# Attention values and router logits in one product per tile beside the shared expert, values kept in DRAM, queries in three half slots

## The reference

```python
xn = layernorm(x)
q = xn @ Wq.T + bq; k = xn @ Wk.T + bk; v = xn @ Wv.T + bv       # per batch
z = softmax(q @ k.T / 16) @ v
gates = softmax(xn @ Wg.T); scores, inds = top_k(gates, 2); scores /= sum(scores)   # 16 experts
y = sum over the two of scores * (silu(xn @ We_gate.T) * (xn @ We_up.T)) @ We_down.T   # hidden 128
shared = (silu(xn @ Ws_gate.T) * (xn @ Ws_up.T)) @ Ws_down.T     # hidden 512
return x + z + y + sigmoid(xn @ Wsg.T) * shared
```

## Time and profile before

| | |
|---|---|
| median of 3 runs | 512.84 us (512.59 to 513.53) |
| the profiled execution | 512.95 us |
| its span | 511.1 us |
| TensorE busy | 503.8 us, 3410 matmuls |
| VectorE, ScalarE, GpSimd busy | 402.7, 279.5, 200.1 us |
| transfers | 71.28 MB, mean 139 GB/s |
| granted TensorE clock | 1.00 in every stretch |

### The profile page before, as it was taken

How to read it: one execution, slowest core, us unless ns; L and a number is a source line. 1 busy time by engine, 2 the same in 40 slices (tenths; PEclk the granted TensorE clock), 3 DMA queues, 4 the chain that set the end, 5 groups by cost and what they waited for, 6 DMA issues and landing times.

```text
span 511.1 us, 10075 instructions
## 1 busy us (share of the span) xinstructions
PE 503.8 (99%) x3410; PEld 462.0 (90%) x3411; DVE 402.7 (79%) x847; ACT 279.5 (55%) x466; POOL 200.1 (39%) x178
## 2 busy tenths in 40 slices
PE   8999999999999999999999999999999999999997
PEld 7898988888989999999999888989989898989986
DVE  5989457899997687777776389897969797888896
ACT  4787885246655464555555547464727364545641
POOL 0001021111005777777770451353554544362730
PEclk9999999999999999999999999999999999999999
DMA  8937176111113565786675730731262213131311
GB/s 311 410 117 280 82 294 233 50 45 39 56 63 114 176 195 182 235 291 195 196 142 148 253 120 25 218 97 53 84 203 98 60 62 84 42 92 32 94 43 63
DMA packets 31185, 71.28 MB, mean 139 GB/s; under 512 B 5312, under 2 KB 9792, under 8 KB 30112
## 3 DMA queue, kind: packets, MB, share of 16 engines
q1 hardware_dynamic: 23840, 51.80, 28.2%
q0 software_dynamic: 6864, 18.75, 14.3%
q10 hardware_dynamic: 432, 0.09, 0.1%
HBM read 43.34 MB, written 27.28 MB: 138 GB/s over the span
## 4 chain that ended last, share of the span: by engine, by line
PE 85%; DVE 7%; issue 4%; DMA 1%; POOL 1%; ACT 1%; POOLq 0%; DVEq 0%
PE ps L805 52%; PE ps L1015 10%; PE ps L945 7%; PE ps L811 6%; PE ps L1047 5%; PE ps L900 1%; PE ps L858 1%; DMA blk_x<-rows,row 1%; POOL rows_y L792 1%; DVE sil L1409 1%; DVE probs_f L1672 1%; PE ps L909 1%; DVE place_hot L1520 1%; DMA rows_y<-ytab,slot 1%; POOL blk_x L762 1%
## 5 line engine op out<-in xcount | busy, mean ns | idle before, releaser
L792 POOL DMA_INDIRECT rows_y<-ytab,slot x64 | 81.0, 1265 | 85.5 <-DVE acc L1687 67.4
L762 POOL DMA_INDIRECT blk_x<-rows,row x79 | 86.0, 1089 | 47.8 <-DVE row L1535 23.3
L805 PE MATMUL ps<-vv,pT 128*128 128x258 f32 x768 | 95.8, 283 | 2.1 <-DVE pT L1331 2.1
L805 PEld LDWEIGHTS ps<-vv,pT 128*128 128x128 f32 x768 | 94.7, 189 | 3.5 <-DVE pT L1331 2.5
L805 PE MATMUL ps<-xT,shared_w 128*128 128x512 f32 x384 | 92.6, 394 | 0.4 <-DVE sil L1409 0.3
L805 PEld LDWEIGHTS ps<-xT,shared_w 128*128 128x128 f32 x384 | 70.7, 188 | 15.5 <-issue 0.8
L805 PE MATMUL ps<-qT,xbT_hi 128*128 128x512 f32 x256 | 79.1, 390 | 0.0
L1015 PE MATMUL ps<-expert_w,blk_xT 128*128 x474 | 66.1, 288 | 0.4 <-DVE blk_xT L1331 0.4
L1015 PEld LDWEIGHTS ps<-expert_w,blk_xT 128*128 128x128 f32 x474 | 59.0, 190 | 0.6 <-issue 0.6
L1319 ACT ACTIVATE probs_f<-probs_f 128x1024 f32<-128x1024 f32 x32 | 33.8, 1056 | 42.6 <-DVE probs_f L1672 42.6
L1125 ACT ACTIVATE scored_t<-ps 128x1024 f32<-128x1024 f32 (+1 forms) x33 | 32.3, 996 | 43.7 <-PE ps L805 39.5
(11 more groups left out here) (166 smaller groups left out, 859.2 us busy)
## 6 DMA issues: line engine op xcount, KB each, us to landing
ytab<-blk_y SPq DMA_DIRECT2D x40, 256.0 KB, 2.7
keys<-xT SPq DMA_DIRECT2D x8, 1024.0 KB, 6.0
stage_e<-in_experts SPq DMA_DIRECT2D x16, 384.0 KB, 3.1
rows<-xn SPq DMA_DIRECT2D x8, 512.0 KB, 3.1
xbT_hi<-keys SPq DMA_DIRECT2D x8, 512.0 KB, 6.1
xbT_lo<-keys SPq DMA_DIRECT2D x8, 512.0 KB, 6.9
out<-acc SPq DMA_DIRECT2D x32, 128.0 KB, 1.7
acc<-in_x SPq DMA_DIRECT2D x7, 512.0 KB, 9.1
```

Source lines behind the costliest of these rows:

```text
L762: e.indirect_dma_start(out=blk_x[:, q, n, :], out_offset=None, in_=rows, in_offset=bass.IndirectOffsetOnAxis(ap=row[:, 2 * b + n:2 * b + n ...
L792: e.indirect_dma_start(out=rows_y[:, r, k, :], out_offset=None, in_=ytab, in_offset=bass.IndirectOffsetOnAxis(ap=slot[:, k, i:i + 1], axis=0),
L805: ins = e.matmul(dst, stationary(p, k), moving(q, k), start=(n == 0), stop=(n == total - 1))
```

## The change

Values and logits come out of one product for each tile of 128 tokens, while the chunk's `xT` is there for the shared expert: the new step `vals` has the tile of `xT` stationary and `value_w` moving, 256 value columns and the router's 18 (16 experts, the shared gate, one for a shift), 274 in all, 6 matmuls into one turn bank. ScalarE copies the 18 logits to their place and the 256 value columns, high part, to `vals_out`; VectorE writes the low part; SP stores both (256 KB) in DRAM. `vals_out` has three places, so ScalarE's copy of a tile waits for the store of the tile three before. `vals_load` brings 2 MB of values per batch into `vv`. What goes: the products `logits`, `logits_turn`, `values_first` and `values` with their copies, remainders and additions, `w_v`, and the clearing of the padded router. New once: `value_w` is split (ScalarE and VectorE, 548 columns), its load of 256 KB stands on SP ahead of the third gate-and-up weight (the load of the same weights late in stage 2 goes).

The queries are kept in three slots of half a batch, so `heads` stands two groups ahead throughout; both halves of batch 0 are made before the first score. In the last two groups the addition of tile 28's rows moves from group 6 into group 7, and two more steps move later. GpSimd's gathers take the bound of their indices from a register that is set once. The DRAM transfers at the start of attention are: shift 0, keys of batch 1 (2 MB), values of batch 0 (2 MB), shift 1, values of batch 1 (2 MB).

```diff
     beside = {
-        0: ([("router_split",), ("root", 1), ("stats", 2)], [("weights_hi", 3), ("invert", 1)], []),
-        1: ([("norm", 1), ("weights_lo", 3)], [("logits", 0)], []),
+        0: ([("root", 1), ("stats", 2)], [("weights_hi", 3), ("invert", 1)], []),
+        1: ([("norm", 1), ("weights_lo", 3)], [("value_split",)], [("keys_store", 0)]),
         2: ([], [("tokens_in", 1)], [("weights_lo", 4), ("weights_hi", 4), ("stats", 3)]),
-        3: ([], [], [("stats", 4)]),
+        3: ([], vals(0, 0, 1), [("stats", 4), ("keys_store", 1)]),
         4: ([("weights_lo", 5)],
-            [("logits", 1), ("logits_turn", 0), ("weights_hi", 5), ("root", 2, 3), ("invert", 2, 3)],
+            [*vals(0, 2, 3), ("weights_hi", 5), ("root", 2, 3), ("invert", 2, 3)],
             []),
-        5: ([("logits_turn", 1), ("best_experts", 0)], [], []),
+        5: ([], vals(1, 0, 1, 2, 3), []),
...
-        13: ([], [("tokens_in", 4)], [("norm", 5), ("expert_split", 1)]),
-        14: ([], [("logits", 4)], []),
-        15: ([("norm", 6)], [("tokens_in", 5)], [("expert_split", 2)]),
-        16: ([], [("tokens_in", 6), ("norm", 7)], []),
+        13: ([], [*vals(3, 2, 3), ("tokens_in", 4)], [("norm", 5), ("expert_split", 1)]),
+        14: ([], vals(4, 0, 1), [("keys_store", 4)]),
+        15: ([("norm", 6)], [*vals(4, 2, 3), ("tokens_in", 5)], [("expert_split", 2)]),
+        16: ([], [*vals(5, 0, 1), ("tokens_in", 6), ("norm", 7)], [("keys_store", 5)]),
...
-    ahead = {1: split("heads", 1, 1), 2: split("heads", 2, 0), 3: split("heads", 2, 1), 4: split("heads", 3, 0),
-             5: split("heads", 3, 1), 6: split("values", 3, 1)}
-    behind = {2: split("values", 1, 1), 3: split("values", 2, 0), 4: split("values", 2, 1), 5: split("values", 3, 0)}
+    ahead = {g: split("heads", *divmod(g + 2, 2)) for g in range(1, GROUPS - 2)}
...
-            steps += [*split("heads", 0, 1), ("heads", 1, 0), ("tops", g), ("heads_split", 1, 0),
-                      ("values", 0, 1), *spread(g), ("values", 1, 0), ("less", new),
-                      ("values_split", 0, 1), ("less", new + 1), *spread_second(g), ("probs", new), ("values_split", 1, 0),
-                      ("less", new + 2), ("probs_hi", new), ("probs", new + 1), ("probs_hi", new + 1), ("probs_lo", new),
-                      ("less", new + 3), ("probs_lo", new + 1), *rows(new + 2), *rows(new + 3)]
+            steps += [("tops", g), *split("heads", 1, 0), *spread(g), ("less", new), ("probs", new), ("less", new + 1),
+                      *spread_second(g), ("probs_hi", new), ("probs", new + 1), ("probs_lo", new), ("less", new + 2),
+                      ("probs_hi", new + 1), ("less", new + 3), ("probs_lo", new + 1), *rows(new + 2), *rows(new + 3)]
...
+                elif kind == "vals":
+                    c, n = a
+                    if (c, n) == (0, 0):
+                        e.wait_ge(value_w_lo, 1)
+                    if n == 0:
+                        e.wait_ge(xT_lo, KD * (c + 1))
+                    product(ps[:, turn_bank(("vals", c, n)), 0:VRC], lambda p, k: xT_of(c)[:, p, k, n * P:(n + 1) * P],
+                            lambda q, k: value_w[:, q, k, :], valued)
...
+                elif kind == "vals":
+                    t = CT * a[0] + a[1]
+                    bank = before[("vals", *a)][0]
+                    e.wait_ge(valued, t + 1)
+                    copied(logits_sb[:, t, :], ps[:, bank, D:VRC], logits_copied)
+                    if t >= VR:
+                        e.wait_ge(vals_stored[t % VR], 16 * (t // VR))
+                    copied(vals_out[:, t % VR, HI, :], ps[:, bank, 0:D], vals_hi)
```

263 lines of the change are left out of this document (115 added, 148 removed).

## The result

The changed kernel takes **519.05 us** (median of 4, 518.05 to 519.70), the kernel before beside it 513.18: ratio **1.0117**, 95% interval 1.0101 to 1.0132. It is slower. The forecast was 513.8, between 508.0 and 518.5: the time lies above the range, by 0.55 at its top, and 5.25 above the middle case.

What follows compares the result with a forecast made beforehand. TensorE, busy 99%, was taken as the bound. Terms -8.7 (work), +6.6 (hand-offs), -0.5 (routing), +3.4 (group 0) and +0.2 (tail) sum to +1.0, giving 513.8 us, range 508.0 to 518.5.

Steps and rivals of the forecast that it cites:

- TensorE's work: Whole kernel: logits, their turns and values go, the 274-column product comes at 0.127 us per matmul; -8.7 us.
- Rival D: New value-and-logit product: 274 columns cost as 258, 1.4 us less, 512.4; a third likely, inside the forecast's case.
- Hand-offs in the shared expert: Shared expert: TensorE waits for banks held until VectorE's remainder is done; +6.6 us, bounds 0 to 13.
- The walk: Shared expert and tail: stepping through the engines' order with measured durations to place and size TensorE's waits; +6.6 in the shared expert.
- Routing and blocks: Routing and start of the blocks: VectorE loses 8 additions and TensorE's small waits may go; -0.5 us, bounds -1 to +2.
- Register: GpSimd's gathers: holding the index bound in a register saves GpSimd's issue at most; 0 us.
- Group 0: Start of attention: TensorE waits 2.7 us for the first pT, plus 0.25 and 0.45 at two hand-offs; +3.4, ends 0 and +5.5.
- The clock: Whole kernel: granted clock taken as 1.00 in every row of stretches, so no term for it.
- Tail: Last groups: shorter group 6 makes score copies of group 7 reach into TensorE; net +0.2 us, bounds -1.5 to +2.
- A: Shared expert, faster: hand-offs hide and the 6.6 falls away, 507.2, or 510.5 if half hidden; chance 0.35.
- B: Start of attention, slower: the burst of 6 MB of loads delays the gathers, 516.5 to 520; chance 0.15.
- C: Two banks and a ring of three too few throughout: stores take 6 us, gaps double to 13, 520.3; chance 0.07.

Runs made afterwards that it cites:

- no_low_read: Changed kernel with the values' low part computed from the high part alone, so a bank is free after ScalarE's copy: 532.90 us, ratio 0.9949 to the kernel before.
- rows_behind: Changed kernel with the row additions of tiles 0 and 1 moved from between group 0's score maxima to behind its last pT: 536.16 us, ratio 1.0017.
- rows_28_back: Changed kernel with tile 28's row additions back at the end of group 6, as before the change: 534.29 us, ratio 1.0035.
- ring_of_two: Changed kernel with two places instead of three for the stored value tiles: 539.42 us, ratio 1.0083.
- cover: rows_behind with the second half of batch 0's heads moved behind group 0's last score, the next heads in their own bank pair: 538.83 us, ratio 1.0079.
- imm_bound: Changed kernel with the gathers' index bound as a constant in each instruction again, instead of a register: 541.12 us, ratio 1.0124.
- combined: Changed kernel with group 3's heads moved into group 0, two chunk 1 tiles behind the first down product, two group 6 row additions later: 533.31 us, ratio 1.0007.

## Why the prediction was wrong

**TensorE's work: right.** -8.7 forecast. At 0.128 instead of 0.127 the new product is 24.6 and not 24.4, so -8.5. Rival D, the price of 258 columns, is out.

**Hand-offs in the shared expert: mechanism right, the term mis-sized.** 6.6 forecast. The stage grew by 22.2, of which 24.6 - 7.3 - 2.8 = 14.5 are work: the hand-offs cost **7.7**. Their idle time is 6.3, as walked; the rest is that a matmul behind a wait does not overlap its predecessor. Between the starts on either side of the wait at 36.32 lie 36.32 - 32.79 = 3.53, which is 1.54 of work, 1.75 of idle time and 0.24 more. Eight times about 0.17. The walk counted idle time alone, and this is its failed term: a restart was put at nothing. The profile books it as busy time of TensorE: -8.5 of work, 1.4 of restarts and 1.6 of slow matmuls (below) make -5.5, and 5.4 less is what the page shows. Of the causes, VectorE's remainder was given too much: no_low_read shows that only 1.2 of the 6.3 goes with it. And the 6.3 against 6.6 is in part luck, since step by step the walk had 0.65 and 2.15 for what measured 0.28 and 1.75, and 0.65 for the 0.36 and 0.94 at 80 and 81.

**Routing and blocks: right in the sum,** -0.7 against -0.5; all of it lies in the blocks, and the routing is within 0.1 of before (73.7 us from the end of the last tile's product to the first block, 73.8 from the end of the last turn of logits before).

**Register: the step that failed for the other chips.** "GpSimd's bound in a register ... so 0" holds on the first chip (blocks 116.7 and 116.0). I argued from GpSimd's busy share, an average over the whole span, while in the blocks stage what TensorE reads next is what GpSimd gathers. On the two of the other chips where it was tested by itself, the same edit is worth about 6 us.

**Group 0: the chain right, the term 0.7 too small.** Before the first weighing the stage has 10.98 us of scores, 2.72 of one head and 5.49 of two pairs of the next scores, so the wait cost 22.8 - 10.98 - 2.72 - 5.49 = 3.6, where I had 2.7. The 0.9 between them is GpSimd being late with a gather, of which rows_behind took 0.8 away. Of the two hand-offs behind it, 0.25 and 0.45 forecast, the first is there with 0.5 (3.39 - 2.88, in the traces at full clock) and the second not. Together 4.1 against +3.4.

**The clock: the step that failed on the first chip.** "No clock enters: it is granted 1.00 in every row" was read from a kernel whose TensorE never stands for more than 1.5 us, and it put the clock at nothing for a kernel with new waits. The change puts 3.2 us of standing into group 0, and the 24 matmuls behind it took 4.50 instead of 2.88, 1.6 more, of which 0.5 only hides the hand-off just counted: **+1.1** net. The median rose by 5.9, the profiled execution, the fastest of its four, by 5.1. For one of the other three a second stretch at the low clock would fit (519.70 us, mean clock 0.993 against 0.996); another took 519.28 at 0.997, so the clock does not explain all of this spread, and there is no trace of it.

**Tail: mis-sized.** From the first weighing on the difference is -11.5; five half batches of values are 5 x 2.87 = -14.4 and the 24 slow matmuls +1.6, which leaves **+1.3** for the tail, where I had +0.2. Its waits came nearly as walked: 1.49, 0.47 and 0.82 against 1.2, 0.25 and 1.1, so 2.8 in all against 2.06 before: +0.7. A restart makes 0.2 more. The help expected from moving tile 28's rows was taken off the walked sum, and 0.4 of the rest are not located. rows_28_back shows that without the move it would have been 1.2 more.

Sum by these: -8.5 + 7.7 - 0.8 + 4.1 + 1.1 + 1.3 = 4.9, against 5.1. Against the forecast's +1.0 that is 3.9 of the 4.1 that were missing: 1.1 each for the hand-offs, the clock and the tail, 0.7 for group 0 and 0.2 for the work, less 0.3 in the other stages. No single term failed alone; two of them, the restart behind a wait and the clock, had been put at nothing. **The rivals:** A (hand-offs hide) is out. B, the burst, can have a part only in the 0.9 us in group 0; that the burst is what made the gather late was not tested (gathers of rows_y land in 3.5, against 3.1 before). C asked for stores of 6 us; they land in 3.5 (median of the page's part 6), and the ring costs at most some tenths at two places, though two places instead of three cost 4.6. The time passed the top of the range by 0.55, less than the clock's 1.1 alone, for which the range held nothing.

The Trainium skill's "Perfetto Trace Analysis" (section Optimization Strategy) ties repeated gaps on the saturated engine to too few buffers. The traces agree in part: the gaps stand in the stretch with two banks and a ring of three, and a ring of two makes them larger (ring_of_two, 9.3 us of waits instead of 6.3); but they do not recur at every pair, only at eight places where another engine is behind. By the Trainium skill's "DMA: Bandwidth & Descriptors" (section Issuing engines are not separate DMA queues) gathers share the DMA engines with SP's loads. The trace shows the row additions waiting 0.63 and 0.74 beside the 6 MB, against 0.69 once before: this does not contradict it and is too little to show it.

## What to carry to other kernels

Before taking work out of the path, list what each piece of it hides: values in attention were hidden nowhere on TensorE, yet they covered the chain of maxima in group 0, and the heads ahead of the first score covered a remainder (cover). A new wait on the saturated engine costs its idle time, some 0.2 us of lost overlap and, if it is long, possibly a stretch at the lower clock; a clock of 1.00 in the kernel before says nothing on that, so it needs a term of its own. And measure a small edit by itself and on more than one chip: where the smallest was tested it was worth about as much, with the opposite sign, as all the rest together, and on the first chip the traces show nothing of it.

## What the runs showed of the hardware that I had not expected

- Before the first weighing the granted clock fell to 0.50 in seven of eight traces with a wait of 3.2 us and behind the 2.42 of rows_behind, but stayed at 1.00 behind 3.19 in imm_bound. Elsewhere it stayed at 1.00 behind 2.59 (cover) and 1.97 (combined). Behind one and the same wait of 1.75 it fell in three traces of ten, and behind none under 1.5. The length of the wait alone does not decide it, and what does is open.
- Chips differ by 4% on the same kernel (513.2 and 532.5 to 535.4 us). By the two traces of the kernel before, all of it lies in the one stage that lives on indirect gathers: 116.7 against 138.9 us, with the other stages within 0.5. At most some 3 of the 22 us are the low clock. Why the rest is slower there is open; GpSimd's rows show the same 1.0 us for each gather on both.
- A gather with its bound in a register instead of a constant shortens the kernel by 6.2 us on a chip of the slower kind, for 79 gathers in that stage, about 0.08 each. What the engine does in that time the profile doesn't show; its "issue" gap of 0.30 between gathers is the same with both.
